# A two-layer transformer with experts on one core: batch 1's statistics for layer 2, the spacing of layer 2's first scatters, and its W1 and W3 loaded expert by expert

## What is computed

```python
h = _layernorm(x) * (1 + ca) + sa
x = x + ga * attention(h)
h = _layernorm(x) * (1 + cb) + sb
x = x + gb * ffn(h)
```

```python
top_v, top_i = jax.lax.top_k(xf @ Wg, 2)
top_w = softmax(top_v)
y = (silu(xf @ W1[e]) * (xf @ W3[e])) @ W2[e]
out = sum(y[top_i] * top_w)
```

## Time and profile before

| | us |
|---|---|
| three runs, median | 945.59 |
| lowest and highest | 942.89, 954.91 |
| the profiled execution | 943.85 |
| its span in the trace | 942.1 |
| PE busy | 834.8 (89%) |
| DVE busy | 720.9 (77%) |
| ACT busy | 546.7 (58%) |
| POOL busy | 282.3 (30%) |
| mean granted clock of PE | 0.897 |

### The profile page before, as it was taken

The page is one execution under the profiler, slowest core; times in us unless marked ns, Lnnn a source line. Parts: engine busy times, 40 slices in busy tenths (PEclk is TensorE's granted clock), DMA queues, the critical chain, the costliest instruction groups (busy, mean ns, idle before and its releaser), DMA issues.

```text
span 942.1 us, 18341 instructions
## 1 busy us (share of the span) xinstructions
PE 834.8 (89%) x6319; PEld 501.3 (53%) x6319; DVE 720.9 (77%) x2077; ACT 546.7 (58%) x1202; POOL 282.3 (30%) x424
## 2 busy tenths in 40 slices
PE   7698999888879869999999999999987989898994
PEld 6354655455579733344344434344432434788994
DVE  5777788887265768898899888989895874786674
ACT  2355656546556524688788868687664765333431
POOL 6233334326412354204210011001025223344332
PEclk9799999998979966799999979799795988988997
DMA  5556523111103133244242403110251100102123
GB/s 156 189 169 195 179 80 108 41 47 36 43 21 96 56 102 125 72 160 145 112 151 69 136 25 105 47 58 25 83 177 51 47 7 21 42 27 78 42 64 113
DMA packets 68470, 82.43 MB, mean 87 GB/s; under 512 B 8295, under 2 KB 44391, under 8 KB 68057
## 3 DMA queue, kind: packets, MB, share of 16 engines
q1 hardware_dynamic: 40120, 46.11, 16.2%
q10 hardware_dynamic: 24960, 28.32, 9.6%
q0 software_dynamic: 3296, 6.82, 2.2%
HBM read 52.08 MB, written 37.80 MB: 95 GB/s over the span
## 4 chain that ended last, share of the span: by engine, by line
PE 55%; DVE 27%; issue 4%; DMA 4%; ACT 4%; POOL 3%; another core or an unknown queue 1%; SPq 1%; ACTq 1%; DVEq 0%; POOLq 0%
PE pv L1898 13%; PE st L1875 10%; DVE M L2199 9%; PE ring L2013 6%; PE ring L1866 5%; PE ring L1769 4%; DVE M L2206 4%; PE st L1998 4%; DVE ring L2203 3%; ACT Et L1623 2%; PE ring L1837 2%; PE st L2006 2%; PE st L1991 2%; PE pv L2006 2%; PE ring L1780 1%
## 5 line engine op out<-in xcount | busy, mean ns | idle before, releaser
L1623 ACT ACTIVATE Et<-st 128x512 f32<-128x512 f32 (+3 forms) x768 | 372.9, 545 | 149.8 <-PE st L1875 130.1
L2206 DVE TENSOR_REDUCE M<-ring 128x1 f32<-128x512 f32 x256 | 159.4, 683 | 29.8 <-PE ring L1866 23.6
L2199 DVE TENSOR_REDUCE M<-ring 128x2 f32<-128x512 f32 x256 | 159.9, 681 | 15.4 <-PE ring L1866 14.7
L1898 PE MATMUL pv<-Et,Va 128*32 128x256 f32 (+3 forms) x1536 | 146.5, 443 | 4.0 <-ACT PVs L1630 2.3
L2203 DVE CUSTOM_DVE_ANT_0 ring<-ring,maskw 128x128 f32<-128x128 f32 (+3 forms) x256 | 120.5, 512 | 36.0 <-PE ring L1866 33.5
L1875 PE MATMUL st<-Qs,Kbd 128*128 128x512 f32 (+3 forms) x256 | 90.0, 370 | 8.9 <-ACT Et L1623 7.5
L1898 PE MATMUL pv<-Et,RV 128*32 128x256 f32 x1024 | 92.4, 434 | 5.1 <-ACT PVs L1630 5.0
L1866 PE MATMUL ring<-Kbd,Qs 128*128 128x128 f32 (+3 forms) x256 | 84.6, 360 | 13.5 <-DVE M L2203 5.9
L1386 POOL TENSOR_SCALAR_AFFINE_SELECT Et<-Et 128x256 f32<-128x256 f32 x128 | 53.0, 419 | 128.0 <-ACT Et L1623 127.7
L1866 PE MATMUL ring<-RKT,Qs 32*128 32x512 f32 x256 | 84.4, 540 | 3.9 <-DVE M L2199 2.3
L1866 PE MATMUL ring<-KT,Qs 32*128 32x512 f32 x256 | 79.0, 553 | 8.9 <-DVE M L2206 8.3
(11 more groups left out here) (303 smaller groups left out, 1337.1 us busy)
## 6 DMA issues: line engine op xcount, KB each, us to landing
Qs<-Dq SPq DMA_DIRECT2D x46, 256.0 KB, 3.0
Xd<-Xd ACTq DMA_DIRECT2D x8, 1056.0 KB, 5.6
Dq<-hq SPq DMA_DIRECT2D x24, 256.0 KB, 3.2
Dk<-hk SPq DMA_DIRECT2D x16, 256.0 KB, 4.1
L1W<-in_L1W ACTq DMA_DIRECT2D x2, 2048.0 KB, 12.6
Kbd<-Dk SPq DMA_DIRECT2D x60, 64.0 KB, 2.0
KT<-Dk SPq DMA_DIRECT2D x15, 256.0 KB, 2.7
Dq<-Xq SPq DMA_DIRECT2D x12, 256.0 KB, 4.3
```

Of the source, the lines that this page charges most:

```text
L1623: e.activation(Et[s // 2 % 4][:, j % 2, q0:512], bank(ph)[:, q0:512], ACT.Exp, scale=SCALE).then_inc(exp_done, 1)
L1898: ins = nc.tensor.matmul(pv[32 * j:32 * j + 32, cols], v, Et[s // 2 % 4][:, j % 2, cols], start=first and (l == 0 or what == "pva"), stop= ...
L2199: e.tensor_reduce(M[i][:, t, j, :], bank(ph)[:, :].rearrange("p (two n) -> p two n", two=2), AX.X, ALU.max).then_inc(mx_red, 1)
L2206: e.tensor_reduce(M[i][:, t, j, 0:1], bank(ph)[:, 0:n], AX.X, ALU.max).then_inc(mx_red, 1)
```

## The change

There are three edits in the plan and what they ask of the waits.

- `("ln", 1)` leaves `STEPS1`. The statistics of batch 1 for layer 2 now stand at the end of `prep_next()`, behind the wait for batch 1's sum, so ahead of `("between",)` and of `leftovers()`.
- `SPREAD[1][0]` goes from 2 to 4: a pair of scatters of layer 2's part 0 every fourth step, so the first at step 455 as before and the last at step 483, where it was 469.
- `layer1_weights()` loads W1 and W3 of one expert at a time, 256 KB each, every seventh step from 430 to about 472, and moves from `prep` to `fast`. The first pair keeps the waits. The first readers, GpSimd's and VectorE's `getw`, wait for all eight.

```diff
-SPREAD = ((2, 2, 1), (2, 3, 1))
+SPREAD = ((2, 2, 1), (4, 3, 1))
...
@@ prep_next
         yield from stage(1, 0, 0)
+        while ("sum", 0, 1) not in flags:
+            yield
+        yield from ln_stats("late1", [1], 3)
...
     def layer1_weights():
-        do("w1")
-        yield
+        for n in range(E):
+            do("w1", n)
+            yield from wait(6)
...
-    prep += [(at["ln", b], ln_stats(f"late{b}", [b], 3)) for b in range(1, NB)]
+    prep += [(at["ln", b], ln_stats(f"late{b}", [b], 3)) for b in range(2, NB)]
...
-                            pool.wait_ge(ld[key], 16)
+                            pool.wait_ge(ld[key], 16 if key == "l1w2" else 16 * E)
...
                 elif what == "w1":
-                    act.wait_ge(pv_half, 2 * before(ph, "pv"))
-                    act.wait_ge(misc_full, before(ph, *MISC))
-                    act.wait_ge(comb_done, before(ph, "combine"))
-                    B = ffns[1]
-                    load("l1w1", B.W1[:, :, :], d["L1W1"].rearrange("e p f -> p e f"))
-                    load("l1w3", B.W3[:, :, :], d["L1W3"].rearrange("e p f -> p e f"))
+                    n, = a
+                    if n == 0:
+                        act.wait_ge(pv_half, 2 * before(ph, "pv"))
+                        act.wait_ge(misc_full, before(ph, *MISC))
+                        act.wait_ge(comb_done, before(ph, "combine"))
+                    load("l1w1", ffns[1].W1[:, n, :], d["L1W1"][n])
+                    load("l1w3", ffns[1].W3[:, n, :], d["L1W3"][n])
```

More of the change, by code:

```diff
@@ L68 @@
           ("blend", 0): 263, ("blend", 1): 391, ("blend", 2): 503, ("rows", 0): 331, ("route", 0): 406, ("route", 1): 522,
-          ("route", 2): 560, "weights": 430, "weights2": 250, "past": 51, ("ln", 1): 1, ("ln", 2): 148, ("ln", 3): 276, ("mod", 0): 100,
+          ("route", 2): 560, "weights": 430, "weights2": 250, "past": 51, ("ln", 2): 148, ("ln", 3): 276, ("mod", 0): 100,
           ("mod", 1): 124, ("mod", 2): 148, ("mod", 3): 172, "wipe": 74, "keys": 84, "first": 480, "experts": 554}
@@ L664, in plan @@
             prep.append((at["blend", b], epi_rec(b, k)))
-    prep += [(at["rows", 0], token_rows(1, 0)), (at["weights"], layer1_weights()), (at["weights2"], layer1_weights2()), (at["past"], past_prep())]
-    prep += [(at["ln", b], ln_stats(f"late{b}", [b], 3)) for b in range(1, NB)]
+    prep += [(at["rows", 0], token_rows(1, 0)), (at["weights2"], layer1_weights2()), (at["past"], past_prep())]
+    prep += [(at["ln", b], ln_stats(f"late{b}", [b], 3)) for b in range(2, NB)]
     prep += [(at["mod", b], modulation(b)) for b in range(NB)]
-    pipeline(1, L1_UNITS, prep, fast + [(4, leftovers()), (at["wipe"], wiping()), (at["keys"], past_keys()),
+    pipeline(1, L1_UNITS, prep, fast + [(4, leftovers()), (at["weights"], layer1_weights()), (at["wipe"], wiping()), (at["keys"], past_keys()),
                                  (at["route", 0], in_turn(slow(token_rows(1, 1)), route(1, 0))),
@@ L2612, in _ @@
                     for key in (("w1", "w2", "b2"), ("l1w1", "l1w3", "l1w2"))[l]:
-                        dve.wait_ge(ld[key], 16 * E if key in ("w1", "w2") else 16)
+                        dve.wait_ge(ld[key], 16 if key in ("b2", "l1w2") else 16 * E)
                     dve.wait_ge(eid_done, n_eid["eid", l, g] + 1)
```

## The result

| | median us | range us | runs |
|---|---|---|---|
| before | 946.32 | 942.89 to 954.91 | 8 |
| changed | 935.18 | 931.45 to 940.46 | 8 |

The changed kernel takes 0.9869 of the time before, with a 95% interval of 0.9827 to 0.9910. That is 1.3% less: the interval leaves out 1, but the difference is under the 2% from which a kernel counts as faster here. The forecast was 935.9 us. The ratios in this document leave out executions more than 1.5% above the fastest of their own kernel, which matters for two kernels: the one with a single addition (945.02, 945.63 and 996.00 us of ten are left out; with the first two back its ratio would be about 0.987) and the third of the last table (932.99, 935.49 and 1046.24 us of six; about 0.978). The profiled execution of the changed kernel took 931.45 us, with a span of 929.7 us.

What follows compares the result with a forecast made beforehand. TensorE (55% of the chain) and VectorE (27%) bound the kernel, with waits at the layer change and layer 2's first scatters. 943.85 - 4.1 - 5.0 + 1.1 = 935.9 us, range 925 to 946 us.

Steps and rivals of the forecast that it cites:

- Both waits named: VectorE's 5.62 us for `rstd` at the layer change; VectorE and ScalarE (7.78 us) standing at layer 2's first scatters.
- The statistics, -4.1 us: Layer change: `rstd` passes the gather on GpSimd, VectorE restarts at 335.54 instead of 339.67 us; bounds 0 and 5.6 us.
- something else of unit 0 or 1 is late by then: Lower bound of the statistics' gain at the layer change: 0 us if other work there is late.
- The scatters, -5.0 us: Layer 2's first scatters: pauses between pairs win back 5.0 of TensorE's 5.7 us lost; bounds 0 and 7.8 us.
- The distance: Layer 2's first scatters: mean distance becomes 1.7 us instead of 1.28 us, next to layer 1's 1.80 us.
- The weights, +1.1 us: ScalarE's queue: eight load pairs at 0.83 us add 5.4 us, a fifth charged; bounds 0 and 5.4 us.
- the third rival: ScalarE's queue: pairs at 1.86 us delay TensorE, loads cost 13.6 us, 948.4 us; decides from 1.3 us a pair; chance 0.07.
- The later last scatter, 0 us: Layer 2's last first-part scatter, issued at about 736 us, still comes 10 us ahead of the read back.
- The first: Rival at layer 2's scatters: pace doesn't matter, so spacing wins nothing; 940.9 us; chance 0.25.
- The second, the clock: Rival: shorter idle keeps TensorE at 2.4 GHz, winning 3.1 us at layer 2's start, then 3.9 behind scatters; 928.9 us; 0.18.

Runs made afterwards that it cites:

- the one with a single addition: The kernel before with one small unused GpSimd addition behind each of layer 2's first sixteen scatters; 935.37 us, ratio 0.9846.
- the third of the last table: The kernel before with moved statistics, wider spacing of the first scatters, one small GpSimd addition behind each second-run scatter; 931.30 us, ratio 0.9760.
- the kernels with additions: The kernel before with small unused GpSimd additions behind each of layer 2's first sixteen scatters: two, 936.59 us, ratio 0.9867; one, 935.37 us, ratio 0.9846.

## Why the prediction was right, point by point

**The number.** 935.9 us came within 1 us of 935.18 us, and part of that is luck. The sum takes 8.0 us off an execution of 943.85 us, which lies 2.5 us below the median of 946.32 us. The measured ratio takes 12.4 us off that median, between 8.5 and 16.4 us. So the reduction was forecast too small, and a low starting point made up for most of it.

**The bound and the place.** The chain stayed where it was. Both waits named were the ones that moved.

**The statistics, -4.1 us.** The hand-over was forecast at 1.49 us and took 1.48 us in both kernels that have the move, so the wait fell by 4.14 us. The bound "something else of unit 0 or 1 is late by then" was real and was taken at nothing: TensorE ran unit 0 at a granted clock of 0.50 instead of 0.67, and VectorE waited 1.8 us more for its banks. About 2.4 us were left at SyncE's next `Qs<-Ms`. Across all profiles the wait usually falls by 2.9 us and 1.8 us are left, since the 5.62 us of the forecast's own execution were a long case. The edit alone measured 5.5 us, with 2.6 to 8.4 us. So the mechanism was right, the term was too large for its place, and its size at the end isn't settled.

**The scatters, -5.0 us.** The cause was right, and it was the step with the least support: it rested on the distance of layer 1's scatters and on two stalls. It overlooked that layer 1 also has a row of four scatters about 1.3 us apart, from 279.98 us, without a stall, as the runs of four in the changed kernel have none. The size was put together wrongly. I took 5.7 us of idle time of TensorE and a bit off. The pair of traces has 3.3 us of idle time, 4.3 us by the clock during the three units, and 2.3 us less in the next block: 5.3 us, near 5.0 us by other terms, which is luck. The kernels with nothing but spaced scatters measured more: 11.5 us, 12.6 us and 14.6 us less, the lowest interval from 7.3 us. So the term was too small, by at least 2 us in time. The profiles agree: the three units take 37.4 to 41.5 us, 39.4 us on average, in the ten without a stall, and 48.3 to 49.9 us, 49.0 us on average, in the three with ten scatters in a row. That is 9.6 us, and the block behind takes 36.7 and 35.8 us on average, so some 8.7 us stay. The profiled execution of before, which the sum goes by, also had a short course further on: its 48.6 us from the second to the third run are the shortest of the ten profiles with a tight second run, 2.5 us below their mean.

**The distance.** Forecast 1.7 us, measured 1.77 us. That pairs inside come without a pause did no harm, nor did a run of four, which the forecast didn't foresee: GpSimd started behind a wait of 7.05 us for TensorE and issued four at once.

**The weights, +1.1 us.** Measured 0.1% slower alone, between 0.25% faster and 0.5% slower, and no difference when taken out. A pair took 1.01 us on average; the third rival's turning point was 1.3 us.

**The later last scatter, 0 us.** Right: it was issued at 718.01 us, and the tiles were read back from 728.65 us on.

**The rivals.** The first is out by the kernels with additions: the pace of GpSimd is what brings the stall and takes it away, though not why. The page "SBUF — State Buffer" of the Trainium skill, section "SBUF: two separate sides", was weighed there as a rule that spacing wouldn't cure; no run here shows GpSimd locked out, since its scatters kept their 0.96 us through the stall. The second, the clock, was right in its second half and wrong in its first. At the scatters the clock rose from 0.72 to 0.92 over the three units. At the start of layer 2 it fell, from 0.67 to 0.50, although TensorE's idle time ahead of it was 2.87 us instead of 7.01 us; the other profiles, above, show the same direction. The third didn't come.

**Beyond the sum.** Single edits multiply to 0.9942 x 0.9879 x 1.0012 = 0.9833; the whole measured 0.9869 and 0.9837. They add up within their intervals, so this doesn't show the edits helping or hindering each other.

## What to carry to other kernels

When an engine stands without a releaser that the trace can name, look at what the other engines issue at that moment: here the remedy was on GpSimd, which no one waited for. Where such a stall stands beside a long row of indirect DMAs, try a pause between them, of 0.57 us here; other work of GpSimd gives it without changing any other engine's list. And a term read from one profiled execution should be checked against others of the same stretch: the wait of 5.62 us was 4.4 us in four others, and the block behind the three units took 30.8 to 37.4 us.

## What was unexpected of the hardware

TensorE's messages to the other engines come late, by up to 7 us, while GpSimd issues scatters 1.27 us apart. ScalarE's wait grows with the length of the run (four 0, six 3.9, eight 5.2 to 6.9, ten 6.6 to 8.2 us). At 1.61 us it is gone. In the kernel before TensorE's transposes ended at 709.60 us and went on with other matmuls, and their reader started at 716.40 us, so what was late was the message and not the work. The code agrees: ScalarE's exponential waits only for `st_full` and `pv_half`, and both come from TensorE. TensorE's own pauses beside the third run say that its issue can be held up as well. GpSimd's eight gathers 1.25 us apart at the change of layer had no such effect. What in a scatter does it, its bytes, its descriptors or its direction, wasn't tried and stays open.

The granted clock of TensorE stayed at 0.50 while it had hardly a pause: 24.89 of 25.00 us busy from 751 us in the changed kernel. The 30 us ahead of that were at 0.97 with 26.43 us busy, and the clock fell in the last 2 us of them, after TensorE had been busy for 3.19 of the last 6 us. In the kernel before, the stretch at 0.50 lay from 707 to 734 us, on and behind the stall, and the block that followed had 0.76. In eleven of the fourteen profiles that block took 37.3 us, with the stall ahead of it (the statistics alone) and without. The Trainium skill ("TensorE: Matmul & The Clock Gate", section "What's actually happening") says that the slow state is the default and that activity releases it; by that rule a TensorE without pauses would be at 2.4 GHz, and the trace doesn't agree: it was at 1.2 GHz for 25 us of unbroken work. What keeps it down stays open. It is part of the spread of all times here: the block took 30.8 us at 0.89 in one execution of the kernel with the spacing alone, 35.0 us at 0.76 before and 37.3 us at 0.66 after, with the same instructions.
